# A transformer block on one core: row maxima turned on VectorE per half of the heads, attention output normalised channel-major and packed by DMA, second score product in 512-column matmuls

## What is computed

```python
ada = silu(c) @ W_ada + b_ada
shift_msa, scale_msa, gate_msa, shift_mlp, scale_mlp, gate_mlp = split(ada, 6)
h = modulate(layernorm(x), shift_msa, scale_msa)
q, k, v = split_heads(h @ W_qkv + b_qkv)           # 16 heads, D = 18
attn = softmax(einsum('blhd,bmhd->bhlm', q * D**-0.5, k))
o = einsum('bhlm,bmhd->blhd', attn, v).reshape(b, l, c)
x = x + gate_msa * (o @ W_proj + b_proj)
h = modulate(layernorm(x), shift_mlp, scale_mlp)
x = x + gate_mlp * (gelu(h @ W_fc1 + b_fc1) @ W_fc2 + b_fc2)
```

## Time and profile before

| quantity | value |
|---|---|
| time, median of 3 runs | 1358.67 us (1358.36 to 1360.45) |
| profiled execution: its own time | 1355.57 us |
| profiled execution: span of the trace | 1353.8 us |
| PE busy | 1286.1 us, 95% |
| PE weight loads (overlap PE) | 1157.0 us |
| ACT busy | 862.6 us, 64% |
| DVE busy | 849.7 us, 63% |
| POOL busy | 478.4 us, 35% |
| granted TensorE clock, mean | 0.992 of full speed |

### The profile page before, as it was taken

How to read it: one execution, slowest core, us unless ns; L and a number is a source line. 1 busy time by engine, 2 the same in 40 slices (tenths; PEclk the granted TensorE clock), 3 DMA queues, 4 the chain that set the end, 5 groups by cost and what they waited for, 6 DMA issues and landing times.

```text
span 1353.8 us, 29365 instructions
## 1 busy us (share of the span) xinstructions
PE 1286.1 (95%) x10995; PEld 1157.0 (85%) x10995; DVE 849.7 (63%) x2086; ACT 862.6 (64%) x1285; POOL 478.4 (35%) x522
## 2 busy tenths in 40 slices
PE   6589999999999999999999999999999999999997
PEld 1477989898998988999989899898989989889886
DVE  5666666666666665666666666666666666666553
ACT  1346667676666767666677766666776667677651
POOL 2102343333333333333333333333343333333344
PEclk9799999999999999999999999999999999999999
DMA  7244333322333433233333323333322334322210
GB/s 229 90 127 126 109 106 128 126 90 89 104 128 106 128 110 103 91 104 119 115 126 107 98 92 113 110 124 126 111 91 96 113 106 128 117 96 83 80 49 23
DMA packets 82935, 146.28 MB, mean 108 GB/s; under 512 B 12486, under 2 KB 51496, under 8 KB 82796
## 3 DMA queue, kind: packets, MB, share of 16 engines
q1 hardware_dynamic: 82796, 144.40, 33.1%
HBM read 96.53 MB, written 47.30 MB: 106 GB/s over the span
## 4 chain that ended last, share of the span: by engine, by line
PE 74%; ACT 10%; issue 5%; DMA 4%; SPq 3%; DVE 2%; POOL 2%; ACTq 0%; POOLq 0%; DVEq 0%
PE a_bank L572 9%; PE score_bank L498 8%; PE x_bank L473 8%; PE st_bank L520 7%; PE turn_bank L531 6%; PE b_bank L586 5%; PE b_bank L588 5%; PE b_bank L587 5%; PE b_bank L572 4%; PE a_bank L553 4%; PE x_bank L481 3%; ACT L680 2%; ACT L647 2%; ACT e L647 2%; PE a_bank L451 2%
## 5 line engine op out<-in xcount | busy, mean ns | idle before, releaser
L820 DVE TENSOR_REDUCE mx<-score_bank 128x2 f32<-128x512 f32 x512 | 340.0, 685 | 101.0 <-PE score_bank L498 99.7
L949 POOL TENSOR_TENSOR gl<-gl_raw,gh 128x512 fp32r<-128x512 f32 (+1 forms) x160 | 188.9, 1181 | 357.8 <-DVE gh L878 357.8
L647 ACT ACTIVATE e<-st_bank 128x1024 f32<-128x1024 f32 x256 | 263.7, 1030 | 50.3 <-PE st_bank L520 49.1
L498 PE MATMUL score_bank<-kl,ql 108*128 108x256 f32 x1024 | 179.5, 297 | 3.5 <-DVE mx L820 1.7
L520 PE MATMUL st_bank<-ql,kl 110*128 110x256 f32 x1024 | 175.6, 293 | 7.0 <-DMA ql<-mxs 4.4
L586 PE MATMUL b_bank<-w,gh 128*128 128x288 f32 x576 | 177.0, 307 | 2.5 <-DVE tmp L884 1.7
L498 PEld LDWEIGHTS score_bank<-kl,ql 108*128 108x128 f32 x1024 | 141.1, 190 | 44.4 <-issue 38.8
L641 ACT CAST mxs<-score_bank 4x256 fp32r<-4x256 f32 x128 | 46.6, 364 | 201.4 <-PE score_bank L508 200.6
L588 PE MATMUL b_bank<-w,gl 128*128 128x288 f32 x576 | 170.1, 295 | 0.0
L587 PE MATMUL b_bank<-w,gh 128*128 128x288 f32 x576 | 170.1, 295 | 0.0
L520 PEld LDWEIGHTS st_bank<-ql,kl 110*128 110x128 f32 x1024 | 139.7, 190 | 10.3 <-DMA ql<-mxs 6.3
(11 more groups left out here) (153 smaller groups left out, 2621.7 us busy)
## 6 DMA issues: line engine op xcount, KB each, us to landing
qk_rows<-qst SPq DMA_DIRECT2D x128, 256.0 KB, 2.5
ql<-qk_rows SPq DMA_DIRECT2D x384, 72.0 KB
kl<-qk_rows SPq DMA_DIRECT2D x384, 72.0 KB
gate<-gates SPq DMA_DIRECT2D x32, 432.0 KB, 3.9
xin<-in_x SPq DMA_DIRECT2D x32, 288.0 KB, 4.4
x<-in_x SPq DMA_DIRECT2D x32, 288.0 KB, 2.8
out<-x SPq DMA_DIRECT2D x32, 288.0 KB, 2.1
qk_rows<-qst SPq DMA_DIRECT2D x32, 128.0 KB, 3.8
```

What stands on the lines that cost most here:

```text
L498: last = nc.tensor.matmul(score_bank[i][:, t * L:(t + 1) * L], ql[0:KH, slot, i, j % HP, t * P:(t + 1) * P], kl[0:KH, slot, j % HP, :], st ...
L647: nc.scalar.activation(e[:, j % 4, :, :, :].rearrange("p i u l -> p (i u l)"), st_bank[:, :, :, :].rearrange("p i u l -> p (i u l)"), ACT. ...
L820: nc.vector.tensor_reduce(mx[:, b % 2, :, col:col + 1], score_bank[i][:, :].rearrange("p (t l) -> p t l", t=NT), AX.X, ALU.max).then_inc(s ...
L949: nc.gpsimd.tensor_tensor(gl[:, cols], g[:, cols], gh[:, cols].bitcast(F32), ALU.subtract).then_inc(g_lo, 1)
```

## The change

1. **Maxima.** The group turns `mt` leave PE and ACT. DVE gathers the maxima of four pairs (half of the heads) in `mx` and turns them with one 32x32-block transpose (`mt` on DVE, 64 elements a row, into `mxt`); eight DMAs per half (`mx_out`) put them into `ql`. So `st(0)` waits for eight DMAs behind `s(3)`, where it waited for two behind `s(1)`.
2. **Attention output.** ACT's copy to `ots`, the PE transposes `on` and `ot`, `onat`, and the copies and splits from `a_bank` go. DVE `on` now works on `turn_bank` channel-major: a stream shuffle spreads row 18 (the sum) over the 32 rows of each head, a reciprocal of 128x256 elements in place, and a multiplication into `on_sb`. `ow` stores that to `o_dram`; six DMAs (`or`) read it back packed, seven heads in each of two tiles of 126 rows, two heads and the bias row in a rest of 119 rows. ACT rounds (`oh`), POOL (`ol`) and DVE (`ol`, the rest) take the low parts. `proj` keeps seven matmuls per tile, over 126, 126 and 119 rows.
3. **Second score product.** `st(j)` is two matmuls of 512 columns instead of four of 256.
4. **Reads of q and k.** 16 DMAs per sample instead of 24, for the same bytes.
5. **Orders.** All five are written anew. A sample's `ln2` steps, `lt` and `fc1` stand one period later than its `proj` (offset -2), the last part of `fc2` at offset -3.

```diff
 PE_ORDER = [
-    ("st", -1, 7), ("s", 0, 3), ("on", -1, 2), ("fc1", -2, 2), ("qk", 1, 1), ("mt", 0, 1), ("st", 0, 0),
...
+    ("lt", -2, 0), ("pv", -1, 2), ("st", -1, 7), ("s", 0, 3), ("fc2", -3, 5), ("lt", -2, 1), ("pv", -1, 3),
...
 SYNC_ORDER = [
...
+    ("store", -4, 0), ("or", -2, 0), ("or", -2, 1), ("or", -2, 2), ("qkr", 0, 7), ("or", -2, 3), ("qkw", 0, 4),
+    ("or", -2, 4), ("or", -2, 5), ("res", -2, 0), ("mx", -1, 1), ("ow", -1, 0), ("ln1_stats", 3, 0), ("qkr", 0, 8),
...
+            def mx_out(b, half):
+
+                sp.wait_ge(mx_turned, HALVES * b + half + 1)
+                slot, _use = half_use(b, half)
                 for i in range(2):
-                    sp.dma_start(ql[KH + i:KH + i + 1, slot, i, j0:j0 + 2, :].bitcast(F32),
-                                 mxs[64 + 2 * i:66 + 2 * i, gr % 2, :].bitcast(F32)).then_inc(mx_rows[gr % 2], 16)
+                    to = ql[KH + i:KH + i + 1, slot, i, :, :].rearrange("p j (t a x) -> p j t a x", t=NT, x=VB)
+                    for a in range(4):
+                        row = VB * a + HP * i
+                        sp.dma_start(to[:, :, :, a, :].bitcast(F32), mxt[row:row + HP, half, :, :]
+                                     ).then_inc(mx_rows[half], 16)
+
+            def ow(b, q):
+
+                sp.wait_ge(turn_drained, QUADS * b + q + 1)
+                if q == 0 and b >= 2:
+                    sp.wait_ge(o_rows[b % 2], 16 * O_READS * (b // 2))
+                sp.dma_start(o_dram[b % 2, q], on_sb[:, q % 2, :]).then_inc(o_stored[q % 2], 16)
+
+            def o_read(b, n):
+
+                if n == 0:
+                    for i in range(2):
+                        sp.wait_ge(o_stored[i], 16 * (QUADS // 2) * (b + 1))
+                    wait(sp, a_full, A_USES * (b - 1) + USE_PROJ + NT)
...
+                if n < 2:
+                    to, src = ol_raw[0:OT, n, :], heads[TH * n:TH * (n + 1)]
+                else:
+                    r0, w0, nr = O_REM[n - 2]
+                    to, src = orem_raw[r0:r0 + nr, :], heads[w0 // D:(w0 + nr) // D]
+                sp.dma_start(to, src).then_inc(o_rows[b % 2], 16)
...
             def st(b, j):
...
-                for i in range(2):
-                    for u in range(NT):
-                        last = nc.tensor.matmul(st_bank[:, i, u, :], kl[0:KM, slot, j % HP, u * P:(u + 1) * P],
-                                                ql[0:KM, slot, i, j % HP, :], start=True, stop=True)
+                for u in range(NT):
+                    last = nc.tensor.matmul(st_bank[:, u, :, :], kl[0:KM, slot, j % HP, u * P:(u + 1) * P],
+                                            ql[0:KM, slot, :, j % HP, :], start=True, stop=True)
...
+            def oh_copy(b, n):
+                act.wait_ge(o_rows[b % 2], 16 * O_READS * (b // 2 + 1))
                 if n == 0:
-                    nc.scalar.copy(xh3[:, :, :].rearrange("p c l -> p (c l)"), a_bank[:, :]).then_inc(o_hi, 1)
+                    wait(act, a_full, A_USES * (b - 1) + USE_PROJ + NT)
+                    nc.scalar.copy(oh[0:OT, :, :], ol_raw[0:OT, :, :]).then_inc(o_hi, 1)
...
+            def mt(b, half):
+
+                for i in range(2):
+                    dve.wait_ge(s_max[i], PAIRS * b + HP * (half + 1))
+                wait(dve, mx_rows[half], 16 * MX_WRITES * b)
+                nc.vector.transpose(mxt[:, half, :, :].rearrange("p t v -> p (t v)"),
+                                    mx[:, half, :, :].rearrange("p t v -> p (t v)").bitcast(F32)).then_inc(mx_turned, 1)
+
             def on(b, q):
 
-                dve.wait_ge(turn_full, TURN_USES * b + 2 * q + 2)
-                o = turn_bank[:, 0:NT * P].rearrange("p (t c v) -> p t c v", t=NT, c=4)
-                nc.vector.reciprocal(rc[:, :, :, :], o[:, :, :, D:D + 1]).then_inc(recip, 1)
-                dve.wait_ge(recip, QUADS * b + q + 1)
-                to = onat[:, :, 4 * D * q:4 * D * (q + 1)].rearrange("p t (c d) -> p t c d", c=4)
-                nc.vector.tensor_tensor(to, o[:, :, :, 0:D], rc[:, :, :, :].broadcast_to([P, NT, 4, D]), ALU.mult
+                dve.wait_ge(turn_full, QUADS * b + q + 1)
+                nc.vector.stream_shuffle(rc[:, :], turn_bank[:, 0:L], [D] * VB).then_inc(on_step, 1)
+                dve.wait_ge(on_step, 2 * (QUADS * b + q) + 1)
+                nc.vector.reciprocal(rc[:, :], rc[:, :]).then_inc(on_step, 1)
+                wait(dve, o_stored[q % 2], 16 * (QUADS // 2 * b + q // 2))
+                dve.wait_ge(on_step, 2 * (QUADS * b + q) + 2)
+                nc.vector.tensor_tensor(on_sb[:, q % 2, :], turn_bank[:, 0:L], rc[:, :], ALU.mult
                                         ).then_inc(turn_drained, 1)
```

More of the change, by code:

```diff
@@ L336, in load_weights @@
                 if kind == "full":
-                    sp.dma_start(to, w[k * P:(k + 1) * P, :]).then_inc(w_loaded[i], 16)
+                    rows = OT if w is w_proj else P
+                    sp.dma_start(to, w[k * rows:(k + 1) * rows, :]).then_inc(w_loaded[i], 16)
+                elif i == I_PROJ:
+                    sp.wait_ge(minus_set, 1)
+                    for r0, w0, nr in O_REM:
+                        sp.dma_start(to[r0:r0 + nr, :], w[w0:w0 + nr, :]).then_inc(w_loaded[i], 16)
+                    for r in O_ONES:
+                        sp.dma_start(to[r:r + 1, :], bias.rearrange("(a n) -> a n", a=1)).then_inc(w_loaded[i], 16)
                 elif kind == "rem":
@@ L962, in sum2 @@
                                         ).then_inc(fc2_added, 1)
-            run(POOL_ORDER, {"ln1_stats": ln1, "ln2_stats": ln2, "xt": xt, "lt": lt, "proj": proj, "bias": bias,
+            run(POOL_ORDER, {"ln1_stats": ln1, "ln2_stats": ln2, "xt": xt, "lt": lt, "ol": ol_sub, "proj": proj,
+                             "bias": bias,
                              "fc1": fc1, "sum2": sum2})
```

226 lines of the change are left out of this document (111 added, 115 removed), and 38 rows, old and new, of tables (ACT_ORDER, DVE_ORDER, PE_ORDER, POOL_ORDER).

## The result

The changed kernel takes 1809.55 us (median of 4 runs, 1808.15 to 1814.37), beside 1358.51 for the kernel before in the same session: a ratio of 1.333, 95% interval [1.330, 1.336]. The prediction was 1318 us and faster. It was wrong by 492 us and in its sign.

A forecast was written before the change was run, and what follows sets the result against it. PE, 98.0% busy, bound the kernel before; afterwards two loops through PE and DVE would set 37.9 us a period. 141.5 + 7 + 29 × 37.9 + 65.5 = 1313 us of span, 1318 us of time; range 1270 to 1366.

The forecast's parts named there:

- The 16 reads instead of 24 save SP about 2.8: On SP's queue: fewer reads of q and k, for the same bytes, save about 2.8 us per sample.
- packed rows come late: Slower rival: ACT's last gelu waits behind `o_rows`; 3 us longer gives period 41, 1407 us; chance of slower 0.13.
- the shuffle: DVE's new 128x256 operation: 0.42 us like a PSUM copy, at most 1.74; called the step most likely wrong.
- the rule of 512 bytes: DMA pieces below 512 bytes cause a read-modify-write; maxima travel as 32 floats, so by it landing would grow.
- PE's own work: PE's work per sample falls from 39.5 to about 36.3 us.
- DVE's new operations: Shuffle, reciprocal and multiplication on DVE: 2.6 us for each quad, 10.4 per sample.
- DVE's total: DVE's work per sample: 25.3 − 2.7 + 10.4 + 0.4 = 33.4 us.
- Loop A: DVE's stretch 22.7 us, PE from `s(5)` through the first `proj` tile 14.3, hand-overs 0.4: 37.4 us.
- Loop B: DVE's stretch, then store, packed reads on SP, ACT's last gelu and PE's `proj`: 37.3 to 38.2 us.
- break-even period of 39.3: Period from which the kernel turns slower, reached if the packed reads' issue and landing take 1.4 us longer.
- The ends: Outside the 29 periods: start 141.5 us plus about 7, drain left at 65.5, with 4 either way.
- Sum: Whole span: 141.5 + 7 + 29 × 37.9 + 65.5 = 1313 us.

The follow-up runs named there:

- a_reads24: The changed kernel with the reads of q and k again as 24 DMAs of 18 rows each; 1416.21 us, ratio 1.0448 to the kernel before.
- a_mx2: The changed kernel with two DMAs for each half's maxima instead of eight, carrying weight constants in 1 KB rows instead of the maxima; 1685.35 us (one run).
- orf_recip8: a24_or_first with the reciprocal over 8 of its 256 elements, the other 248 left out; 1337.06 us (one run).
- a24_or_first: a_reads24 with the store issued on SP behind the six reads of the packed rows instead of ahead of them; 1405.64 us, ratio 1.0345 to the kernel before.

## Why the prediction was wrong

**The step that failed** is the sentence "The 16 reads instead of 24 save SP about 2.8". It counted issues and bytes. The bytes are the same, but a read whose outermost dimension is 2 is carried by two engines and holds up what follows in the queue: 2.5 to 7.3 us for the q and k store, 3.67 to 9.15 for the maxima. Nor is anything saved on SP. In the changed kernel, then in a_reads24, issues of this line:

```profile
L422 SPq DMA_DIRECT2D kl<-qk_rows x120: 438/615/3326, 611.9 to 1393.1; - x120
```

```profile
L419 SPq DMA_DIRECT2D kl<-qk_rows x240: 272/339/1442, 401.6 to 1199.7; - x120
```

A large read takes about 0.62 us to issue instead of 0.33, and two of the small ones a sample are held for about 2.3 behind the large ones. Summed over all of them it is 12.7 us a sample against 8.4: a cost of 4.3 where the sum had a saving of 2.8. The rival "packed rows come late" had the mechanism and its place, ACT's `oh` ahead of the exponentials, but not the cause, and it allowed 3 us more where `oh` waits 8.3 us a sample and 2.7 in a_reads24. Against it stood "each part of the path has a row"; the trace of before had reads of 18 rows only, and the new shape had none. It should have got bounds from both sides, as the shuffle did. Of what the Trainium skill states in "DMA: Bandwidth & Descriptors" the prediction weighed the rule of 512 bytes, which did not decide: in a_mx2 the maxima's pieces are 256 floats long, not 32, and the store still lands in 7.3 us. The rule that decided stands there too, and I passed it over.

The same shape is left in part 2: two of the six reads of the packed rows take two heads of 18 rows (36 KB each), in every run of the changed kernel. What they cost was not tested.

Point by point, for what was left when part 4 is undone:

- *PE's own work.* 36.3 predicted; 36.6 in orf_recip8 (PE busy 771.56 of 800 us, period 37.97). Right.
- *DVE's new operations.* 2.6 us for a quad; 2.7 measured. The shuffle, called the likeliest to be wrong, was right: 0.447 from 0.42.
- *DVE's total.* 33.4 predicted, 35.7 in a_reads24 (707.45 of 800 us busy, times 40.42). Missing were mainly the stretched SBUF operations: the rows shown above give 5 × 0.12 + 2 × 0.74 + 2 × 0.25 = 2.6 us a sample.
- *Loop A.* 37.4 predicted, 40.0 measured. To the last maximum of `s(4)`, where I ended DVE's stretch, it is 24.8 instead of 22.7 us, and what is left of the 39.99 is 15.2 instead of 14.7 with the hand-overs. The link that binds, `sum2` to `b_bank`, was in the order and I did not follow it.
- *Loop B.* 37.3 to 38.2 predicted; the period is 40.42 in a_reads24. One term is 5.6 us of issues on SP instead of 3.2, since the reads of the packed rows take 0.31 to 0.81 us and not each the 0.35 of a q or k read. That this loop mattered is shown by a24_or_first, which takes the store out of it and gains 0.43 us a period. The break-even period of 39.3 was worked out with the predicted ends; with those of a_reads24 it is (1353.8 − 172.6 − 69.8)/29 = 38.3, and the repaired kernel lies above both.
- *The ends.* Start 141.5 + 7 predicted, 172.6 in a_reads24 (207.8 in the changed kernel); end 65.5 predicted, 69.8. So 28 us were missing here, as much as 1 us a sample. Why the start is so much longer was not tested; from 100 to 140 us PE is busy for 29.5 us at a granted clock of 0.83 in a_reads24, and for 38.5 of 41.5 us at 1.00 before.
- *Sum.* For a_reads24 172.6 + 29 × 40.42 + 69.8 = 1414.6, its span (1414.5). Of the 101 us to the predicted 1313, 73 are the period and 28 the ends. Even without the reads in two runs, "faster" would have been wrong.

Open: why the start is 24 us longer than predicted, and whether a better order for DVE and SP, with both loops cut at once, would bring the repaired kernel under the one of before. Neither was tried.

## What to carry to other kernels

When DMAs are merged, look at the shape of what results and not only at their number: two, or a count like 34 with no larger divisor up to 16, as outermost dimension made small reads hold up a whole queue, and the price showed as a longer landing of their neighbours. In a pipeline with in-order engines find the links of every loop that passes the engine that grows; taking 2.6 us of work away outside the loop's stretch brought nothing, 0.42 inside it brought about as much, and when two loops are equally long, shortening one of them alone pays little. Measure parts alone: part 3 was a gain of 0.42% buried in a change that cost 33%.
